# Output normalisation without a mean: centred output weights and biases in a transformer block (Trainium2, one core)

## The reference

```python
x = x + layernorm(attention(layernorm(x)))
x = x + layernorm(ffn(layernorm(x)))

def layernorm(x, eps=1e-05):          # over the last axis, no scale, no shift
    m = mean(x); v = var(x)
    return (x - m) / sqrt(v + eps)

attention(x): qkv = x @ qkv_w.T + qkv_b    # 16 heads of 16
    q, k = rope(q), rope(k)
    scores = q k^T * 16**-0.5, causal mask, softmax
    return (softmax(scores) @ v) @ proj_w.T + proj_b
ffn(x): P = x @ U1                         # 256 -> 64
    H = gelu(P @ V1 + b1)                  # 64 -> 1024
    Q = H @ U2                             # 1024 -> 64
    return Q @ V2 + b2                     # 64 -> 256
```

## Time and profile before

| | |
|---|---|
| median of 3 runs | 1206.66 us (1205.65 to 1210.28) |
| profiled execution | 1208.03 us |
| its span, first to last instruction | 1206.3 us |
| mean granted TensorE clock | 0.992 |
| busy: PE, DVE, ACT, POOL | 1155.2, 941.1, 941.8, 658.8 us |

### The profile page before, as it was taken

One profiled execution on the slowest core, in us unless ns is written; L12 is line 12 of the kernel. 1 busy time (PEld: TensorE's weight loads), 2 busy tenths in 40 slices (PEclk: granted clock), 3 DMA queues, 4 the chain that ended last, 5 costly groups with the idle time before them and its releaser, 6 DMA issues.

```text
span 1206.3 us, 25813 instructions
## 1 busy us (share of the span) xinstructions
PE 1155.2 (96%) x9844; PEld 619.4 (51%) x9844; DVE 941.1 (78%) x1458; ACT 941.8 (78%) x1898; POOL 658.8 (55%) x718
## 2 busy tenths in 40 slices
PE   5899999999999999999999999999999999999995
PEld 4655446544654456445654564455545554454542
DVE  6998786789678886888678958896888886476666
ACT  4477878788868877887878877887788689678785
POOL 2467325944495349633874387346844343336647
PEclk9899999999999999999999999999999999999998
DMA  6586544665555745576367636762766443402413
GB/s 202 180 143 127 106 66 79 159 130 103 111 140 132 133 81 142 128 107 140 93 147 104 144 81 152 115 151 37 177 117 127 100 96 114 131 1 92 154 54 122
DMA packets 99259, 142.22 MB, mean 118 GB/s; under 512 B 24896, under 2 KB 60992, under 8 KB 99136
## 3 DMA queue, kind: packets, MB, share of 16 engines
q1 hardware_dynamic: 99136, 140.58, 51.9%
HBM read 79.70 MB, written 51.38 MB: 109 GB/s over the span
## 4 chain that ended last, share of the span: by engine, by line
PE 63%; DMA 9%; SPq 8%; DVE 8%; POOL 7%; ACT 3%; issue 2%; DVEq 0%; POOLq 0%; ACTq 0%
PE PV L875 16%; PE RING L857 12%; PE RING L822 10%; PE RING L776 6%; DMA QK<-split_parts 4%; PE RING L886 3%; PE RING L789 3%; PE RING L927 3%; SPq L649 3%; PE RING L920 3%; SPq L624 2%; DVE MB L1015 2%; PE RING L828 2%; DMA X<-x 2%; ACT PB L1206 2%
## 5 line engine op out<-in xcount | busy, mean ns | idle before, releaser
L1206 ACT ACTIVATE PB<-RING 128x512 f32<-128x512 f32 (+2 forms) x1280 | 623.5, 566 | 139.4 <-PE RING L857 130.9
L1015 DVE TENSOR_REDUCE MB<-RING 128x2 f32<-128x1024 f32 (+2 forms) x448 | 497.0, 1142 | 96.1 <-PE RING L828 48.1
L857 PE MATMUL RING<-QK 64*128 64x512 f32 (+3 forms) x1536 | 320.5, 395 | 1.5 <-DMA QK<-NSROW 0.9
L1301 POOL TENSOR_SCALAR_AFFINE_SELECT PB<-PB 128x512 f32<-128x512 f32 x256 | 160.9, 638 | 275.1 <-ACT PB L1206 274.7
L822 PE MATMUL RING<-QK 62*128 62x512 f32 (+3 forms) x1536 | 296.2, 387 | 14.2 <-DMA QK<-split_parts 8.7
L857 PEld LDWEIGHTS RING<-QK 64*128 64x128 f32 x1536 | 169.2, 186 | 156.1 <-ACT PB L1206 92.3
L1015 DVE TENSOR_REDUCE M<-RING 128x2 f32<-128x768 f32 (+1 forms) x186 | 191.3, 1041 | 56.1 <-PE RING L828 55.3
L875 PE MATMUL PV<-PB,VL 128*32 128x512 f32 (+3 forms) x2048 | 224.1, 522 | 0.5
L822 PEld LDWEIGHTS RING<-QK 62*128 62x128 f32 x1536 | 156.7, 186 | 126.8 <-DVE MB L1015 36.3
L828 PE MATMUL RING<-MASKK,MASKQ 64*128 64x128 bf16 (+1 forms) x768 | 112.5, 248 | 0.0
L1231 ACT ACTIVATE F_H<-RING,F_B 128x512 f32<-128x512 f32 x128 | 80.5, 687 | 18.6 <-PE RING L920 18.5
(11 more groups left out here) (141 smaller groups left out, 1507.8 us busy)
## 6 DMA issues: line engine op xcount, KB each, us to landing
QK<-split_parts SPq DMA_DIRECT2D x372, 128.0 KB, 5.8
split_parts<-PARTS SPq DMA_DIRECT2D x60, 256.0 KB, 3.1
split_parts<-EO SPq DMA_DIRECT2D x60, 256.0 KB, 3.6
ATT<-OT SPq DMA_DIRECT2D x128, 64.0 KB
INV<-inverse_sums SPq DMA_DIRECT2D x32, 256.0 KB
block_mid<-Y SPq DMA_DIRECT2D x16, 512.0 KB, 4.4
F_X<-block_mid SPq DMA_DIRECT2D x16, 512.0 KB, 5.6
out<-F_Y SPq DMA_DIRECT2D x32, 256.0 KB, 2.1
```

Source lines behind the costliest of these rows:

```text
L857: ins = e.matmul(m[:, i, :], QK[g % 3][r, 1, k, 128 * j:128 * j + 128], QK[g % 3][r, 0, k, 512 * c + off:512 * c + 512], start=True, stop= ...
L1015: e.tensor_reduce(acc, ring(("max", g, s, u), pairs, n), AX.X, ALU.max).then_inc(v_max, 1)
L1206: e.activation(buf[:, h, pairs[0]:pairs[-1] + 1, :], strip(("score", g, s, u), pairs, n), ACT.Exp).then_inc(a_exp, 1)
L1301: e.affine_select(buf[:, :, 0:128], buf[:, :, 0:128], pattern=[[0, 4], [1, 128]], base=0, channel_multiplier=-1, compare_op=ALU.is_ge, fil ...
```

## The change

A row y = a W + b has the mean over its columns equal to a w + β, where w is the mean over the columns of each row of W and β the mean of b. If w is subtracted from the rows of W and β from b, every output row has mean zero. This is done once in the kernel, on DVE: for the projection's weights and bias (centre) and for V2 and b2 (f_centre). The output normalisation is then a multiplication with the scale alone. The variance is still taken from the statistics.

- First normalisation: y_rows on ACT goes. POOL multiplies two tiles at a time with the scale (y_scale) ahead of each residual.
- Second normalisation: f_norm goes. The residual takes over the scaling: on DVE for a = 1 (and three of four in the last part) in one instruction per tile, on POOL for the others as a multiplication and an addition.
- y_pow and f_ypow lose the negated mean and the product.
- proj waits for the six steps of centre, f_y for the five of f_centre.
- The orders of all engines and the banks are other strings. PE has the same steps but for two heating matmuls (h) that go.

```diff
 def taken_by(engine, step):
-    if what in ("f_norm", "f_res"):
-        last = at[0] == NB - 1 and at[2] == int(what == "f_norm")
-        return (engine == "DVE") == last
+    if what == "f_res":
+        return engine == res_by(*at)
     return True
+def res_by(i, js, a):
+    return "POOL" if (a == 0 if i < NB - 1 else (js, a) == (HALVES[0], 1)) else "DVE"
...
                 elif what == "proj":
                     w.wait_ge(g_att, NTH["att_scale", b, c, 1])
+                    w.wait_ge(v_cen, 6)
...
+                elif what == "centre":
+                    w.wait_ge(o_mi["fold"], 1)
+                    e.tensor_reduce(MEAN[:, 0:2], WP[:, :, :], AX.X, ALU.add).then_inc(v_cen, 1)
+                    e.tensor_reduce(MEAN[:, 2:3], BP[:, :], AX.X, ALU.add).then_inc(v_cen, 1)
+                    w.wait_ge(v_cen, 2)
+                    e.tensor_scalar(MEAN[:, 0:3], MEAN[:, 0:3], -1.0 / D, None, ALU.mult).then_inc(v_cen, 1)
+                    w.wait_ge(v_cen, 3)
+                    for k in range(2):
+                        e.tensor_scalar(WP[:, k, :], WP[:, k, :], MEAN[:, k:k + 1], None, ALU.add).then_inc(v_cen, 1)
+                    e.tensor_scalar(BP[:, :], BP[:, :], MEAN[:, 2:3], None, ALU.add).then_inc(v_cen, 1)
...
# VectorE
                 elif what == "f_res":
+                    w.wait_ge(f_ypow, NTH["f_spread", i, js])
+                    for j in js:
+                        r = 4 * a + j
+                        ins = e.scalar_tensor_tensor(y[:, a, j, :], y[:, a, j, :], YF[i % 2][3][:, r:r + 1], X1[i % 5][:, a, j, :],
+                                                     ALU.mult, ALU.add)
+                    ins.then_inc(f_resv, 1)
...
# ScalarE
-                elif what == "y_rows":
-                    e.activation(YS[c][:, j, :], YS[c][:, j, :], ACT.Identity,
-                                 scale=YRS[c][:, j:j + 1], bias=YNM[c][:, j:j + 1]).then_inc(a_yn, 1)
-                elif what == "f_norm":
...
# GpSimd
-                    e.tensor_scalar(YNM[c][:, :], YMV[c][:, :, 0], -1.0, None, ALU.mult).then_inc(g_yve, 1)
...
-                    e.tensor_tensor(YNM[c][:, :], YNM[c][:, :], YRS[c][:, :], ALU.mult).then_inc(g_ynm, 1)
+                elif what == "y_scale":
+                    b, c, j0 = at
                     w.wait_ge(g_yrs, NTH["y_dev", b, c])
+                    scale = YRS[c][:, j0:j0 + 2].unsqueeze(2).to_broadcast([128, 2, D])
+                    e.tensor_tensor(YS[c][:, j0:j0 + 2, :], YS[c][:, j0:j0 + 2, :], scale, ALU.mult).then_inc(g_ysc, 1)
                 elif what == "residual":
-                    w.wait_ge(a_yn, NTH["y_rows", b, c, 3])
+                    w.wait_ge(g_ysc, NTH["y_scale", b, c, j0])
...
                 elif what == "f_res":
+                    scale = YF[i % 2][3][:, 4 * a + js[0]:4 * a + js[-1] + 1].unsqueeze(2).to_broadcast([128, 2, D])
+                    e.tensor_tensor(y[:, a, rows, :], y[:, a, rows, :], scale, ALU.mult).then_inc(f_ysc, 1)
+                    w.wait_ge(f_ysc, NTH[step])
                     e.tensor_tensor(y[:, a, rows, :], y[:, a, rows, :], X1[i % 5][:, a, rows, :], ALU.add).then_inc(f_res, 1)
```

More of the change, by code:

```diff
@@ L81, in steps_by_name @@
         "load_x": [(b,) for b in range(2, NB)],
-        "ln_stats ln_rows y_stats y_rows": [(b, c, j) for b, c in halves for j in range(4)],
+        "ln_stats ln_rows y_stats": [(b, c, j) for b, c in halves for j in range(4)],
         "ln_dev ln_pow y_dev y_pow store": halves,
@@ L104, in steps_by_name @@
         "proj": [(b, c, q) for b, c in halves for q in range(4)],
-        "proj_out residual": [(b, c, q) for b, c in halves for q in (0, 2)],
-        "first_turn first_turn_out first_low first_shift fold_weights fold fold_out f_load f_zero f_fill f_weights f_rest": [()],
+        "proj_out y_scale residual": [(b, c, q) for b, c in halves for q in (0, 2)],
+        "first_turn first_turn_out first_low first_shift fold_weights fold fold_out centre f_centre f_load f_zero f_fill f_weights f_rest": [()],
         "f_stats f_pow f_rows": [(n,) for n in range(2 * NB)],
@@ L114, in steps_by_name @@
         "f_spread f_ypow": [(i, js) for i in parts for js in HALVES],
-        "f_norm f_res f_store": [(i, js, a) for i in parts for js in HALVES for a in (1, 0)],
+        "f_res f_store": [(i, js, a) for i in parts for js in HALVES for a in (1, 0)],
         "f_next": [(i,) for i in range(5, NB)],
@@ L142 @@
     "ACT": dict(l="ln_rows", x="xt_out", q="qk_out", r="round", v="values_out", t="chain_turn_out", e="exp",
-               o="ot_copy", y="y_rows", w="w_high", T="f_turn_out", g="gelu", Q="q_out", n="f_norm", F="first_turn_out"),
+               o="ot_copy", w="w_high", T="f_turn_out", g="gelu", Q="q_out", F="first_turn_out"),
     "DVE": dict(x="xt_low", q="w_low", s="ln_stats", d="ln_dev", r="rope", l="rest", w="fold_weights", f="fold_out", m="max_out",
                i="att_inverse", p="proj_out", S="y_stats", D="y_dev", W="f_weights", F="f_stats", R="f_rows",
-               U="f_u1_out", Y="f_y_out", P="f_spread", N="f_norm", A="f_res", a="chain_max", b="chain_low",
-               X="first_low"),
-    "POOL": dict(p="ln_pow", o="ones", r="rope", l="rest", s="select", a="att_scale", P="y_pow", R="residual",
+               U="f_u1_out", Y="f_y_out", P="f_spread", A="f_res", a="chain_max", b="chain_low",
+               X="first_low", c="centre", C="f_centre"),
+    "POOL": dict(p="ln_pow", o="ones", r="rope", l="rest", s="select", a="att_scale", P="y_pow", y="y_scale", R="residual",
                f="f_pow", F="f_ypow", A="f_res"),
@@ L161 @@
[L161 to L165, removed]
@@ L227 @@
+        "hagaahLtIhaaaamobRatmobSSNSSSNStSSStNSSSSSSSSSSSSSSSSSSSSSSS"
     ),
@@ L732, in sync @@
                     i, = at
-                    w.wait_ge(f_res, max(NTH["f_res", i - 5, js, a] for js in HALVES for a in range(2)))
+                    for a in range(2):
+                        w.wait_ge(f_resv if a else f_res, max(NTH["f_res", i - 5, js, a] for js in HALVES))
                     load_f(i)
@@ L736, in sync @@
                     i, js, a = at
-                    w.wait_ge(f_resv if i == NB - 1 and a == 0 else f_res, NTH["f_res", i, js, a])
+                    w.wait_ge(f_resv if res_by(i, js, a) == "DVE" else f_res, NTH["f_res", i, js, a])
                     rows = slice(js[0], js[-1] + 1)
```

246 lines of the change are left out of this document (118 added, 128 removed).

## The result

The changed kernel took 1220.74 us (median, 1218.76 to 1223.99), the kernel before 1206.16 us beside it on the same chip. The ratio is 1.0118, with a 95% interval of 1.0081 to 1.0155: slower by some 14 us, where 1200 us had been forecast. The profiled execution took 1218.76 us, its span is 1217.0 us.

A forecast was written before the change was run, and what follows sets the result against it. Attention was taken as bound by a ring of PE, ACT and DVE, PE first, and PE nearly full in feed-forward; -4.8 + 0.5 + 0.2 - 1.1 + 0 - 1.8 = -7.0 us gave 1200 us, range 1190 to 1210.

The forecast's parts named there:

- Rival 3: Feed-forward stage: DVE bounds it, f_rows and f_u1_out come 2 us late in each of six parts; 1212 us, chance 0.13.
- Rival 1: Attention: PE's order and DVE bound it, stalls stay and only change name; about -3 us, 1203.7, chance 0.22.
- ACT's rows, -4.8: Attention: without normalisation rows among ACT's exps, PE's waits for ACT shrink in proportion; -4.8 us, bounds 2.0 to 33.6.
- rival 2: ACT was the limit, chiefly in attention, as judging PE by busy weight loads suggests; some 15 us gained, 1192, chance 0.17.
- POOL's scaling, +0.5: Attention: 32 scalings on POOL delay selects that PE waits for, priced by POOL's added load; +0.5 us, bounds 0 to 5.
- Centring, +0.2: Attention: centring done once on DVE, about 2.2 us of work covered by DVE's slack; +0.2 us, at most 2.2.
- Fewer switches, -1.1: PE's order: steps of another kind follow at 1771 places instead of 1792; -1.1 us, between 0 and 2.3.
- Feed-forward stage, 0 (-2 to +12): Feed-forward stage: ACT's relief, -1.3 us, balances DVE's added residual steps, +1.3 us; together 0.
- Tail, -1.8: Last part: shorter path from DVE's first touch to the end, 13.2 us instead of 15.1; -1.8 us (-1.4 to -2.4).
- The signs named: Whole kernel: expected busy times, L1206 waits of 80 to 90, PE over 99% busy from 1050 to 1150; L1082 or L1093 waits refute.

The follow-up runs named there:

- run 7: Kernel before without the first output normalisation's rows on ACT (y_rows), nothing in their place: 1208.47 us, 1.0007.
- run 12: Kernel before without y_rows on ACT, with the 32 scalings on POOL ahead of the residuals, no centring: 1222.46 us, 1.0131.
- Run 11: Kernel before with centre added behind the 88th maximum and proj waiting for it, nothing else changed: 1210.17 us, 1.0026.
- run 6: Kernel before with the attention half alone: centre behind the 88th maximum, y_scale on POOL ahead of each residual, no y_rows: 1222.32 us, 1.0120.
- run 9: Changed kernel with the feed-forward stage's orders and banks taken from the kernel before plus the feed-forward half alone: 1209.5 us, 1.0022.
- run 5: Kernel before with the feed-forward half of the change alone (f_centre, residual split between DVE and POOL), in the old orders: 1207.2 us, 0.9991.
- run 1: Changed kernel with centre moved in DVE's order from behind the 60th maximum to behind the 88th: 1226.28 us, 1.0129.
- run 10: Changed kernel with centre in five pieces, behind maxima 68, 72, 76, 80 and 84: 1221.58 us, 1.0120.
- runs 2 and 3: Changed kernel, feed-forward parts 0 to 6, leaving out POOL's scaling and addition (1214.58 us, 1.0028), or DVE's residual instruction (1212.02 us, 1.0023).
- run 4: Changed kernel, feed-forward parts 0 to 6: ACT scales both halves without bias, POOL adds, DVE's 14 residual steps go: 1216.0 us, 1.0057.
- 13 and 14: Changed kernel with feed-forward strings of the feed-forward-half-alone kernel for DVE and POOL only (1224.15 us, 1.0149), or for PE, ACT, SP and banks only (1222.39 us, 1.0131).
- run 8: Kernel before with V2 and b2 centred, ACT scaling without bias in parts 0 to 6, and the changed kernel's tail: 1205.74 us, 0.9977.

## Why the prediction was wrong, step by step

The forecast was -7.0 us; +14 were measured. Rival 3 (slower, 0.13) named the stage and almost the size, 12 us on the sum, but not the whole cause. Rival 1's own sum was also off: tail, half of the switches and the added load, -1.8 - 0.55 + 0.7, give -1.7 us and not -3.

**ACT's rows, -4.8: wrong, it is nothing that can be measured.** Run 7 has it in the old orders: 1.0007, and the interval leaves a gain of 1.8 us at most. The step that failed is "if PE's waits for ACT shrink in proportion". PE's loads still waited as long for the bank that an exp empties; the waits went from 92.3 to 93.1 us when the rows went. The four rows found on the chain at 523 to 527 us were there, but a place on the chain is no gain: rival 1, the stalls stay, is what happened here, only that they kept their name too: the waits of L822's loads (L821 there) for DVE's maxima are 51.2 us with the rows and 51.6 without. The Trainium skill (Perfetto Trace Analysis, Identifying the Most-Contended Engine), weighed as rival 2, pointed at ACT and DVE; run 7 does not agree for ACT.

**POOL's scaling, +0.5: the worst mis-sized term.** Each cost less than assumed (1.04 us in place of 1.28), and yet run 12 gives 1.0131 (0.91 to 1.71%), some 16 us in the old orders (11 to 21), three times the upper bound of 5. The step priced the average share of selects that PE waits for. What counts is the worst place: a y_scale and a residual together hold POOL for 2.3 us, a select behind them holds the product, and PE's string stands (longest wait 2.5 us, 0.6 before). That reading is the trace's; no run placed the scalings differently in the old orders. Runs 11 and 12 add up to 19 us where run 6 has both and lost 14, which their intervals allow. The changed kernel's new attention orders have room for it: there the wait for selects is 11.6 us and attention ends 1.2 us late. By the ratios of runs 9 and 5, which differ in attention alone, 1.0022 less 0.9991, the attention half costs 0.31% or 3.7 us in the new orders (0 to 7, with both intervals) and 14 us in the old ones (run 6). So the new orders give some 10 us back in attention; that gain was in no term of the sum.

**Centring, +0.2: too small at least by a factor of five.** Run 11 gives 3 us (1 to 5). "The cover is attention's slack on DVE" failed: DVE has spare time on average but not 2 to 4 us in one piece at that place, because the maxima behind it feed PE. Two of its instructions were also blocked beside POOL's rope (L1045 took 1.11 us for 128x3 elements, and 0.17 in run 1 away from the rope; the two L1048 1.59 and 1.04), and the clock fell after PE's stand of 1.3 us. In the changed kernel this local loss is made up by the 481st exp, and neither moving (run 1) nor splitting it (run 10) gained anything in all.

**Fewer switches, -1.1: not measured.** Nothing here separates it. The new orders as a whole are worth far more than the count of switches, with a plus in attention and a minus behind it.

**Feed-forward stage, 0 (-2 to +12): the sign of the case was missed.** The durations of a residual instruction were about as foreseen: 0.48 us without POOL's pair (0.35 to 0.45 forecast), 0.85 on average, and 2.66 us for the two at 1201.78; DVE went from 66% to 76% in 1050 to 1150 where 79% was said. What was not foreseen is what that load costs. In the old orders it costs nothing (run 5, 0.9991); in the new ones 10 us, of which 7 go when either partner is left out (runs 2 and 3), 4 when ACT takes DVE's step (run 4), and 8 when the stage's strings are those of run 5 (run 9; 11.6 by the ratios). Runs 9, 13 and 14 together say that it is the fit of the strings. The step that failed is to price the stage by DVE's load, 79% and so 1.3 us, where one stand of PE of 6.0 us and the low clock behind it made most of the loss. A second path had no term at all: the loads of input parts now wait for residual steps in DVE's string (1122.05 us, 1112.93 before). How much of the hole is due to it, no run tells. The rule weighed there (the Trainium skill, SBUF — State Buffer, Who interferes with whom: a VectorE instruction with two SBUF inputs and a GpSimd instruction that reads SBUF contend, and one waits for the other) agrees with the trace, 477 ns without POOL's two instructions and 846 with them. It says nothing of the kernel's time: in run 5 the step is blocked too, 636 ns, and the ratio is 0.9991.

That a late DVE string holds PE until 1142.6 us is seen in the chain above. Which pair of letters is at fault was not tried, and whether the new orders were made for shorter durations of DVE is a guess.

**Tail, -1.8: right in the mechanism.** From the first touch to the end 12.6 us (13.2 forecast, 15.1 before). Only 0.8 us came through from the last matmul on, since the residual of part 6 made DVE late; with ACT scaling that part (run 8) 2.3 us did.

**The signs named.** ACT's busy time was 886 (875 forecast), POOL's 676 (690), DVE's 972 (960), all near. The waits for L1206 did not fall; PE fell to 86% from 1100 to 1150 us; PE waited for L1121, the second line of f_u1_out, which had been named as the mark of a wrong prediction.

## What to carry to other kernels

Before an engine is relieved, leave its work out and put nothing in its place: one run showed that 37.6 us of ACT were worth 1.8 us at most, where the forecast from the waits had been 4.8. Work added to an engine with a fixed order is priced by the longest piece in which it keeps that engine from what PE is about to need, not by the engine's load: 2.3 us at a time on a POOL that is busy 55% cost some 16 us here, 2 to 4 us once on DVE some 3. When orders change along with the work, run the new work in the old orders before judging either, stage by stage. And when a step moves to another engine, look at which loads wait for it to free a buffer.

## What the runs showed of the hardware

- POOL's multiplication of 128x512 by a broadcast column took 1.04 us; its addition of two full tiles of that size 1.28 us.
- ACT's pass over 128x256 took 507 ns with a scale alone and 596 ns with scale and bias.
- A DVE instruction of 128x3 elements took 1.11 us beside POOL's rope and 0.17 us otherwise: being small doesn't save an instruction from being held up.
- Where PE had stood for 6.0 us (until 1142.59), 1.3 us (until 122.29) and, in run 11, 2.5 us (until 160.68), the granted clock was 0.66, 0.68 and 0.67 over 1140 to 1150, 120 to 130 and 160 to 170 us, means of its two levels of 2.4 and 1.2 GHz. So such a stand cost more than it lasted. Not each did: after 1.7 us in run 9 (until 1114.07) the clock stayed at 1.00.
